# First norm by ScalarE and GpSimd, gates as rounded products, earlier bank choices and a last batch by row tiles in a decoder block with gated cross-attention

## The reference, cut to what matters

```python
# x (16, 256, 256), ctx (16, 77, 256)
h = layernorm(x + multihead(x, x, x, ..., causal=True), ln1_g, ln1_b)          # 16 heads of 16
h = layernorm(h + multihead(h, ctx, ctx, ..., causal=False), ln2_g, ln2_b)
h = layernorm(h + relu(h @ w1.T + b1) @ w2.T + b2, ln3_g, ln3_b)               # 1024 hidden
qp = h @ Wq + bq; kp = ctx @ Wk + bk; vp = ctx @ Wv + bv                       # one head of 256
y = softmax(qp @ kp.T / 16) @ vp
gate = concat(qp, y) @ Wg + bg
out = h + y * mask * sigmoid(gate)
# layernorm(z) = g * (z - mean) / (std + 1e-6) + b, std over d - 1
```

## Time and profile before

| what | value |
|---|---|
| median of 3 runs | 816.09 us (814.78 to 816.56) |
| the profiled execution's own time | 814.99 us |
| its span, first to last instruction | 812.6 us |
| mean granted TensorE clock | 0.978 |
| PE / PEld / DVE / ACT / POOL busy | 94% / 77% / 68% / 64% / 57% |

### The profile page before, as it was taken

One profiled execution on the slowest core, in us unless ns is written; L12 is line 12 of the kernel. 1 busy time (PEld: TensorE's weight loads), 2 busy tenths in 40 slices (PEclk: granted clock), 3 DMA queues, 4 the chain that ended last, 5 costly groups with the idle time before them and its releaser, 6 DMA issues.

```text
span 812.6 us, 19616 instructions
## 1 busy us (share of the span) xinstructions
PE 762.6 (94%) x7072; PEld 624.1 (77%) x7072; DVE 550.9 (68%) x1221; ACT 517.4 (64%) x1224; POOL 460.0 (57%) x582
## 2 busy tenths in 40 slices
PE   6998999999999998889699999999999999999986
PEld 4786778888877776556467889888888888988864
DVE  4435777878788988866878666686668544663453
ACT  5432466656565556555777888888777887855542
POOL 2403477767767676563346566656565588556330
PEclk9999999999999999896979999999999999999998
DMA  9687677987577674344322222222220100011132
GB/s 286 173 262 183 148 135 126 157 138 133 106 132 132 103 110 99 83 115 99 72 58 56 57 57 57 57 53 57 55 46 7 46 2 6 27 56 50 50 96 79
DMA packets 105304, 76.49 MB, mean 94 GB/s; under 512 B 43261, under 2 KB 101967, under 8 KB 104947
## 3 DMA queue, kind: packets, MB, share of 16 engines
q1 hardware_dynamic: 101850, 72.36, 41.7%
q10 hardware_dynamic: 3360, 2.90, 1.2%
HBM read 25.49 MB, written 11.42 MB: 45 GB/s over the span
## 4 chain that ended last, share of the span: by engine, by line
PE 51%; issue 14%; DVE 11%; POOL 10%; ACT 5%; DMA 1%; ACTq 0%; POOLq 0%; DVEq 0%
PE a_misc L89 11%; PE a_s L1039 5%; PE a_pair L89 5%; POOL c_hidden L1979 4%; PE a_pair L827 4%; PE a_s L803 4%; PE a_pair L845 4%; PE a_s L801 3%; PE a_pair L1126 3%; PE a_pair L1138 3%; DVE a_nm L1480 2%; PE a_s L1097 2%; DVE c_z L1590 1%; PE a_pair L999 1%; PE a_pair L848 1%
## 5 line engine op out<-in xcount | busy, mean ns | idle before, releaser
L1205 ACT ACTIVATE a_pT<-a_pair 128x512 f32<-128x512 f32 x192 | 113.7, 597 | 79.8 <-PE a_pair L827 72.4
L1979 POOL TENSOR_TENSOR c_hidden<-c_hid,c_hidden 128x256 fp32r<-128x256 f32 x128 | 94.5, 738 | 120.6 <-ACT c_hidden L1369 120.5
L1480 DVE TENSOR_REDUCE a_nm<-a_s 128x2 f32<-128x512 f32 (+1 forms) x192 | 126.9, 677 | 44.8 <-PE a_s L803 44.2
L1039 PE MATMUL a_s<-c_w,c_hidden 128*128 128x256 f32 x768 | 118.4, 293 | 0.7 <-DVE res L1731 0.7
L1335 ACT ACTIVATE a_pT<-a_pair 77x512 f32<-77x512 f32 x128 | 75.2, 589 | 64.4 <-PE a_pair L984 63.7
L1886 POOL TENSOR_SCALAR_AFFINE_SELECT a_pT<-a_pT 128x256 f32<-128x256 f32 (+1 forms) x192 | 91.4, 495 | 21.8 <-ACT a_pT L1205 21.4
L89 PE MATMUL a_pair<-c_fxh,c_w 128*128 128x256 f32 x512 | 99.9, 288 | 1.0 <-ACT c_hid L1361 1.0
L1039 PEld LDWEIGHTS a_s<-c_w,c_hidden 128*128 128x128 f32 x768 | 99.0, 190 | 1.7 <-issue 1.4
L1655 DVE TENSOR_REDUCE a_nm<-a_s 128x5 f32<-128x385 f32 (+1 forms) x96 | 55.3, 577 | 50.6 <-PE a_s L961 50.4
L89 PEld LDWEIGHTS a_pair<-c_fxh,c_w 128*128 128x128 f32 x512 | 79.3, 191 | 1.2 <-ACT c_hid L1361 1.2
L827 PE MATMUL a_pair<-a_sq,a_sk 98*128 98x256 bf16 (+1 forms) x512 | 75.1, 250 | 4.4 <-ACT a_pT L1205 3.7
(11 more groups left out here) (259 smaller groups left out, 1984.1 us busy)
## 6 DMA issues: line engine op xcount, KB each, us to landing
a_sq<-a_parts SPq DMA_DIRECT2D x96, 128.0 KB, 4.3
a_sk<-a_parts SPq DMA_DIRECT2D x96, 128.0 KB, 4.3
a_sq<-c_parts SPq DMA_DIRECT2D x96, 128.0 KB
x<-in_xT SPq DMA_DIRECT2D x16, 256.0 KB, 5.0
res<-in_x SPq DMA_DIRECT2D x16, 256.0 KB, 5.2
out<-g_fin SPq DMA_DIRECT2D x16, 256.0 KB, 2.1
a_sk<-kc_parts SPq DMA_DIRECT2D x96, 38.5 KB
g_vv<-vv_rows SPq DMA_DIRECT2D x16, 154.0 KB
```

Source lines behind the costliest of these rows:

```text
L1039: last = mt(down[:, qt * D:(qt + 1) * D], (hh, hl)[x](m)[:, qt * P:(qt + 1) * P], w2(y, m), start=m == 0 and qt == 0 and i == 0, stop=m == ...
L1205: nc.scalar.activation(pT[g % NPT][:], stps[g % 2][:], ACT.Exp).then_inc(s_exp, 1)
L1480: nc.vector.tensor_reduce(nm[c % 2][:, QT * heads[0] + qt:QT * heads[-1] + qt + 1:QT], sps[g % 2][:].rearrange("p (h k) -> p h k", h=len(h ...
L1979: nc.gpsimd.tensor_tensor(hl(m), hid[n % NHID][:], f32(hh(m)), ALU.subtract).then_inc(c_hl, 1)
```

## The change

The first norm becomes: DVE forms nmr1 = -mean/std for whole groups of batches at once, ACT does (res/std + nmr1) in one instruction per row tile, POOL multiplies by ln1_g, POOL adds ln1_b. The eight `weight_low` move from DVE to POOL. The gates are formed by `mm3` from a high and a low part of `gx` and of `wqg`. ACT and DVE make the parts of `gx`; the scores still use F32 `gx`. The stored gate weights double in size. `cross_values` alternates banks for its first seven groups. `LONE_H` and `LONE_XO` become 7 and 9. The last batch is mixed, gated, finished and stored by row tile.

```diff
@@ context_products
+            dve.wait_ge(s_wqgh, 1)
+            nc.vector.tensor_tensor(wqg[:, 1, :, :], two(fps[0]), f32(wqg[:, 0, :, :]), ALU.subtract).then_inc(s_wqgl, 1)
@@ banks
-    ND, GV, LONE_H, LONE_XO = 3, 4, 9, 11
+    ND, GV, LONE_H, LONE_XO = 3, 4, 7, 9
+    mixed_bank = lambda m: avps[m % 2] if m < SOLO_A else av_ps          # SOLO_A = 7
@@ PE cross_values
-                    atleast(pe, c_tr, rr // 2)
+                    atleast(pe, c_tr, m - 1 if m < SOLO_A else m)
@@ PE gates
+                pe.wait_ge(g_xl, c + 1)
                 for qt in range(QT):
-                    for kt in range(KT):
-                        last = mt(xo(c)[:, qt * 2 * D + D:(qt + 1) * 2 * D], gx[c % 3][:, kt, qt * P:(qt + 1) * P], wqg[:, kt, :],
-                                  start=kt == 0, stop=kt == KT - 1)
+                    last = mm3(nc.tensor, xo(c)[:, qt * 2 * D + D:(qt + 1) * 2 * D],
+                               lambda x, kt: (gxh, gxl)[x][c % 2][:, kt, qt * P:(qt + 1) * P], lambda y, kt: wqg[:, y, kt, :], range(KT))
@@ ACT
+            def first_normed(c):
+                act.wait_ge(c_nmr, 1 + (c >= B // 2) + (c >= B - 4))
+                atleast(act, c_h, c)
+                for qt in range(QT):
+                    n = QT * c + qt
+                    last = nc.scalar.activation(z1[:, qt, :], t.res[:, n, :], ACT.Identity, scale=t.rstd[:, n:n + 1], bias=nmr1[:, n:n + 1])
+                last.then_inc(c_zr, 1)
...
-                    centred_scale(n + 3, z1, c_zr, c_z, t.rstd)      # cross unit 1
+                if s == 6 and n > -4 or s == 7 and n == -4:
+                    first_normed(n + 4)
...
+                nc.scalar.activation(gxh[c % 2][:], gx[c % 3][:], ACT.Copy).then_inc(g_xh, 1)     # gated unit 3
@@ DVE
-                if s == 3:
-                    centred(n + 4)
-                if n in (-1, 0, 2, 3) and s in (3, 7):
-                    weight_low((-1, 0, 2, 3).index(n) * 2 + s // 7)
+                nc.vector.tensor_tensor(gxl[c % 2][:], gx[c % 3][:], f32(gxh[c % 2][:]), ALU.subtract).then_inc(g_xl, 1)   # gated unit 0, batch e - 1
@@ POOL
+                nc.gpsimd.tensor_tensor(z1[:], z1[:], ln1[0].unsqueeze(1).broadcast_to([P, QT, D]), ALU.mult).then_inc(c_weighted, 1)
...
                 if s == 0:
                     cross_o_low(n - 3)
+                    if n == -3:
+                        weighted_rows(0)
+                    shifted_rows(n + 3)
-                if s == 2:
-                    shifted_rows(n + 3)
...
+                if s == 7 and n > -4:
+                    weighted_rows(n + 4)
+                if n in (-1, 0, 2, 3) and s in (6, 7):
+                    weight_low((-1, 0, 2, 3).index(n) * 2 + s - 6)
@@ the last batch
+            def last_rows(qt):                                             # DVE, per row tile: gate, then finish
+                dve.wait_ge(g_fact, B + qt)
...
+            for qt in range(QT):
+                sp.wait_ge(g_fin, B + qt)
+                sp.dma_start(out[B - 1][:, qt, :], fin[(B - 1) % 2][:, qt, :]).then_inc(stored[(B - 1) % 2], 16)
```

More of the change, by code:

```diff
@@ L134, in context_products @@
     wkq = [sb(f"wkq{i}", [P, KT, D], F32R) for i in range(2)]
-    wqg = sb("wqg", [P, KT, D], F32)
+    wqg = sb("wqg", [P, 2, KT, D], F32R)
     parts = nc.alloc_sbuf_tensor_at("x_parts", [P, 3, B, KT, SC], BF16, offset=t.place["a_sq1"])
@@ L387, in _ @@
             act.wait_ge(s_wqg, 1)
-            nc.scalar.activation(wqg[:], two(fps[0]), ACT.Copy).then_inc(s_wqgc, 1)
+            nc.scalar.activation(wqg[:, 0, :, :], two(fps[0]), ACT.Copy).then_inc(s_wqgh, 1)
             for i in range(NTOK):
@@ L541, in causal_cross_feed_gated @@
     rootc = sb("rootc", [P, 3], F32)
-    rstd2 = sb("rstd2", [P, NT], F32)
+    rstd2, nmr1 = sb("rstd2", [P, NT], F32), sb("nmr1", [P, NT], F32)
     sps = [ps(f"s{i}", 512) for i in range(2)]
@@ L583, in causal_cross_feed_gated @@
     gvv = [gat(f"vv{i}", [SCE, 2 * D], F32, *p) for i, p in enumerate((("a_sq0", 0), ("a_sq0", half), ("a_sq1", 0)))]
-    wqg = gat("wqg", [P, KT, D], F32, "a_sq1", half)
-    gx = [gat(f"x{i}", [P, KT, S], F32, *p) for i, p in enumerate((("a_sq2", 0), ("a_sq2", 2 * quarter), ("a_sq3", 0)))]
+    wqg = gat("wqg", [P, 2, KT, D], F32R, "a_sq1", half)
+    gx = [gat(f"x{i}", [P, KT, S], F32, "a_sq2", i * quarter) for i in range(3)]
+    gxh, gxl = ([gat(f"{n}{i}", [P, KT, S], F32R, *p[i]) for i in range(2)]
+                for n, p in (("xh", (("a_sq2", 3 * quarter), ("a_sq3", 0))), ("xl", (("a_sq3", quarter), ("a_sq1", quarter)))))
     gate = [gat(f"gate{i}", [P, QT, D], F32, "a_sq3", (2 + i) * quarter) for i in range(2)]
@@ L778, in _ @@
                 sp.dma_start(gvv[c][SC:SCE], d.row).then_inc(g_row, 16)
-            sp.dma_start(wqg[:].rearrange("p k c -> p (k c)"), d.wqg).then_inc(g_wqg, 16)
-            for c in range(B):
+            sp.dma_start(f32(wqg[:].rearrange("p x k c -> p (x k c)")), d.wqg).then_inc(g_wqg, 16)
+            for c in range(B - 1):
                 if c + ND < B:
@@ L1446, in gate_tanh, with gate_tanh_last @@
                 nc.scalar.activation(gate[c % 2][:], xo(c)[:].rearrange("p (q c) -> p q c", q=QT)[:, :, D:2 * D], ACT.Tanh, scale=0.5).then_inc(g_fact, 1)
+            def gate_tanh_last(qt):
+                act.wait_ge(g_xo, B + qt)
+                atleast(act, g_gated, B - 2)
+                nc.scalar.activation(gate[(B - 1) % 2][:, qt, :], xo(B - 1)[:, qt * 2 * D + D:(qt + 1) * 2 * D], ACT.Tanh,
+                                     scale=0.5).then_inc(g_fact, 1)
             def gated_slot(e, k):
@@ L1451, in gated_slot @@
                         gated_one()
-                    gate_tanh(e - 2)
+                    if e - 2 < B - 1:
+                        gate_tanh(e - 2)
+                    if e - 2 == B - 1:
+                        for qt in range(QT):
+                            gate_tanh_last(qt)
                     p_copy(e - 1)
@@ L1580, in causal_slot @@
                     residual(n - 3)
-            def centred(c):
-                if not real(c):
-                    return
-                if c == 0:
-                    dve.wait_ge(s_xl, B - 1)
-                atleast(dve, c_h, c)
-                for qt in range(QT):
-                    n = QT * c + qt
-                    nc.vector.scalar_tensor_tensor(z1[:, qt, :], t.res[:, n, :], t.mv[:, n, 0:1], ln1[0], ALU.subtract,
-                                                   ALU.mult).then_inc(c_z, 1)
             def centred2(c):
@@ L1693, in cross_turn_av @@
                 atleast(dve, c_on, n)
-                nc.vector.transpose(tr[0][:], av_ps[:]).then_inc(c_tr, 1)
+                nc.vector.transpose(tr[0][:], mixed_bank(n)[:]).then_inc(c_tr, 1)
                 dve.wait_ge(c_tr, n + 1)
@@ L1798, in shares, with gated_x_low @@
                                         ALU.mult).then_inc(g_p, 1)
+            def gated_x_low(c):
+                if not real(c):
+                    return
+                if c == 0:
+                    stacks_dead(dve, 3)
+                dve.wait_ge(g_xh, c + 1)
+                atleast(dve, g_gates, c - 1)
+                nc.vector.tensor_tensor(gxl[c % 2][:], gx[c % 3][:], f32(gxh[c % 2][:]), ALU.subtract).then_inc(g_xl, 1)
             def gate_x(c):
@@ L1839, in gated_slot @@
                         gated_constants()
-                    finish(e - 3, 0)
+                    if e - 3 < B - 1:
+                        finish(e - 3, 0)
+                    if e - 3 == B - 2:
+                        finish(e - 3, 1)
                 if k == 1:
-                    gate_x(e - 2)
+                    if e - 2 < B - 1:
+                        gate_x(e - 2)
+                    if e - 2 == B - 1:
+                        for qt in range(QT):
+                            last_rows(qt)
                     gated_maxes(e)
-                if k == 2:
+                if k == 2 and e - 3 < B - 2:
                     finish(e - 3, 1)
@@ L1847, in gated_slot @@
                     shares(e)
+                if k == 0:
+                    gated_x_low(e - 1)
             for stage, n, s in order:
```

100 lines of the change are left out of this document (69 added, 31 removed).

## The result

The changed kernel takes 809.61 us, the median of five executions (804.25 to 810.47), beside 816.09 before: a ratio of 0.9908, with a 95% interval from 0.988 to 0.9935. Over all of them the mean is 808.4 (11 executions), against 817.3 for the kernel before (76): 9.0 us faster, where 20 had been forecast. Beside the kernel before in the same comparison the means differ by 7.6 in the first and by 9.7 in the second.

What follows compares the result with a forecast made beforehand. PE bounds the kernel, except where causal and cross slots interleave (261 to 450 us), where PE waits mostly for DVE. Stretch -15.0 (-11.0 - 2.0 - 8.0 + 6.0), gates -3.5, end -1.5: -20.0, so 796 us; range 784 to 812, own range 787 to 804.

Steps and rivals of the forecast that it cites:

- rival A: Interleaved stretch: DVE not the bound, freed time becomes waits for scores and exponentials; banks give 4; 810 us; chance 0.18.
- The DVE work that goes: Interleaved causal and cross slots (261 to 450 us): removed DVE instructions end 11.0 of PE's 16.5 us waits; bounds 4, 16.5.
- ACT: Same interleaved stretch: a third of the 6.1 us that PE waits for ACT's exponentials goes, 2.0; bounds 0 and 4.
- The clock: Same stretch: lost clock falls like PE's idle time, 55% of 15.1 us, so 8.0 come back; bounds none and 12.
- The POOL work: Same stretch: POOL's new multiplies and low parts (24.4 us of work) cost 6.0 us; bounds 1 and 14.
- The two joints I named: Cross slots -1 and 0, units 6 and 7: POOL's queued work makes PE wait 2 us at each.
- The cross slots after it: Cross slots without causal ones, after the interleaved stretch: PE full, still 21.0 us each, no change forecast.
- caught chains: Interleaved stretch: new POOL instructions slow some of DVE's short chains, 2.0 us, part of the 6.0 for POOL.
- The gates: Gate products: 0.29 us less per batch, none at batch 10; 3.5 us taken in all; bounds 1 and 4.6.
- The wait for `g_xl` at batch 10: Batch 10's gates: wait for the new low part replaces the wait for g_gated, so that batch gains nothing.
- The end: From the last mix to the end: half-size finishes save 1.1 us, smaller last store 0.4; sum -1.5, bounds 0.6 and 2.2.
- Context part, XO and H banks: Context part's extra subtract and DRAM traffic: nothing, 1 us if uncovered; the bank changes LONE_XO and LONE_H: no gain.

Runs made afterwards that it cites:

- e13: Kernel before with only the first norm changed and POOL's multiply by its weight left out: 805.56 us, ratio 0.986.
- e15: Changed kernel without POOL's multiply by the first norm's weight and with the weight low parts back on DVE: 805.77 us, ratio 0.9851.
- e9: Changed kernel with POOL's multiply by the first norm's weight left out: 806.29 us, ratio 0.9862.
- e3: Kernel before with only the two alternating banks for the first seven products with the values: 815.62 us, ratio 0.9977.
- e12: Changed kernel with the first norm back on DVE and ACT as before: 812.61 us, ratio 0.9948.
- e6: Changed kernel with POOL's weight multiply at cross unit 0 of its own slot and the bias at unit 2: 805.25 us, ratio 0.9846.
- e4: Kernel before with only the gates changed: three rounded products, their high and low parts, LONE_H 7 and LONE_XO 9: 814.61 us, ratio 0.9972.
- e10: Changed kernel with the weight multiply at unit 0, the last deviation chain behind the shares, batch 13's second row tile finished earlier: 801.38 us, ratio 0.9813.
- e1: Kernel before with only the first norm changed, POOL's weight multiply included: 812.35 us, ratio 0.9935.
- e2: Kernel before with only the eight weight low parts moved from DVE to POOL: 814.40 us, ratio 0.9964.

## Why the prediction was wrong

The direction held, and so did the places; the size was more than twice what came. The measured 809.61 lies within 784 to 812 only because that range was drawn out to take in rival A's 810; it is outside the forecast's own 787 to 804. By its steps:

- **The DVE work that goes: the failed step.** "I take two thirds of 16.5, 11.0." With nothing new on GpSimd DVE's waits fell by 4.6 and 5.2 (e13, e15, with L1590 gone) and PE's idle time by 5.9 and 5.6; by 6.5 with the low parts gone too (e9). The bound of a quarter (4) was nearer than the value taken. The nine waits on the maxima are queues on DVE, as I read them, but six of them stand behind other work: over all of DVE's 16.5, the trace of before has a removed instruction in front of 7.1. Of what went, 2.2 (e15) came back at the next instruction that PE needs from DVE. The 4.0 at the banks was inside the relief as I had it: in e13, with one bank, it fell to 1.0. The new banks alone (e3) end it too, but there the turn of the cross maxima waits instead.
- **ACT: about right.** 2.0 were forecast; its waits fell by 1.5 (e13) and 2.4 (e15).
- **The clock: right for the relief, wrong for the whole.** 8.0 were forecast, and 8.0 came back in both runs without GpSimd's new work. In the whole 5.4 came back in the mean of three profiles, 7.9, 2.3 and 6.1 one by one; that the new waits let it fall again is likely, but the same kernel scatters by more than the difference. The step that tied it to idle time in proportion (55% less idle, 55% less clock loss) fails in form: idle fell by a quarter and the clock's loss by half. In e3 the idle time rose by 2.3 and the loss fell by 5.7. What the dips hang on instead is not shown.
- **The POOL work: right in size as far as one profile tells,** 6.0 forecast, 5.1 measured (2.6 of them through the clock), net of what DVE gained by the low parts' leaving. The two joints I named were not the ones: the worst is cross slot 3, units 6 and 7, where I had the products "two units or more ahead of their users". They are, but DVE is not. POOL and DVE in the first profile:

```profile
386.52 1.27 POOL L2045 TENSOR_TENSOR c_w<-c_raw,c_w 128x512 fp32r<-128x512 f32 x1
387.75 1.26 POOL L1984 TENSOR_TENSOR c_z<-c_z,ln_g 128x512 f32<-128x512 f32 x1
388.97 1.27 POOL L2045 TENSOR_TENSOR c_w<-c_raw,c_w 128x512 fp32r<-128x512 f32 x1
```

```profile
386.71 1.10 DVE L1649 TENSOR_SCALAR a_var<-mv 128x2 f32<-128x2 f32 x1
387.85 1.19 DVE L1651 TENSOR_SCALAR a_root<-a_var 128x2 int32<-128x2 int32 x1
388.95 0.43 DVE L1734 STREAM_TRANSPOSE a_o<-a_on 128x256 f32<-128x256 f32 x1
389.41 0.28 DVE L1712 TENSOR_TENSOR a_mT<-a_misc,a_mT 32x128 bf16<-32x128 f32 x1
```

  Each of the two tiny instructions ends with POOL's (0.15 and 0.17 at 525, where POOL is idle), and L1712, for which PE waits 2.4, is two places behind. The same wait of 2.4 stands in e9 and e12, which have the low parts on POOL and no multiply.
- **The cross slots after it: 1.3 more, forecast at nothing.** "Cross slots still 21.0" held for all but the one from 10 to 11, where the multiply meets the deviation chain (e6). The forecast's 2.0 for caught chains was for the stretch alone.
- **The gates: right where they were costed, absent elsewhere.** 0.29 for each of nine batches (e4). The six at the end gave nothing, where I had taken 0.9 off for all together; so 2.5 in the tail, not 3.5. The wait for `g_xl` at batch 10 came as written, at 2.4. That the clock may fall behind it was not in the sum; it is 0.7 to 1.0 us from batch 9's gates to batch 15's, and most of why gates and end together gave 2.5 in the whole and not 3.5.
- **The end: -1.0 for -1.5.** From the last mix to the end 8.3 became 7.3. The missing 0.5 is a wait of 0.63 of batch 15's first `fin` for the store of batch 13, whose second row tile is finished only behind `gate_x` of batch 14; with that moved up it is 6.7 (e10), 1.6 less, as forecast.
- **Context part, XO and H banks:** nothing, as forecast; between the first landmark and that of causal batch 11 the changed kernel is 0.3 shorter.

In sum: forecast -15.0, 0, -3.5 and -1.5; measured -8.4, +1.3, -2.5 for gates and end, and -0.3 ahead of it all, -9.9 from single profiles where the means differ by 9.0. Of the rivals A came nearest in its number (810), but not in its mechanism: the banks gave 1.4 rather than 4, and DVE's relief was real. (That DVE itself waits for L803 and L961, which A has from the earlier trace rows, does not stand in those rows; the view of DVE's waits has it, 6.0 and 15.2 from 261 to 450.)

The rule of the Trainium skill cited in the prediction ("GPSIMD Engine Reference") names as victims VectorE instructions with two SBUF inputs or in a 2-port performance mode. The 0.95 above is of the first kind; the 1.10 and 1.19 have one input, and whether they ran in such a mode no row shows. By that rule alone the move would have been a loss; the runs make the new norm a gain of 4 to 5 us (e12, e1), its price on GpSimd included.

Left open: why e2's time fell by 2 to 3 us where its profile shows 1.2; the share of the low parts in the 5.1; and what decides how far the clock falls, since the same kernel's stretch scatters by 5.6 us through it.

## What to carry to other kernels

A wait that an engine ends is not relief just because that engine gets less to do: look in the timeline at what the engine did before the instruction that ends the wait, count only waits with the work that goes in front of them, and expect a part of them to come back at the next instruction that is needed. When elementwise work moves to GpSimd, look at which tiny VectorE instructions stand in a chain beside its new place, since each may grow from 0.16 to 1.2 us; another unit of the same slot was worth 2.9 us here (e6). On TensorE the same wait of 2.4 to 2.6 us was followed by no fall of the clock in one profile and by 13 us at its lower level in another, so take several executions, and cut the span at fixed pieces of work, before a difference of a few us is put down to a change.

## What the runs showed of the hardware

A 128x2 VectorE instruction that runs 0.15 to 0.17 us alone took 1.10 and 1.19 beside two-input GpSimd instructions of 1.27, and ended when these did, although these two (`TENSOR_SCALAR`) have one input. In the kernel before, 40 VectorE instructions of 128x2 or 128x8 (reductions and aggregates left out) took over 0.6 us, and in the changed kernel 44; each of them ends within 0.04 us of a GpSimd instruction's end.

After the same wait of 2.4 to 2.6 us before batch 10's gates TensorE's granted clock stayed at 2.4 GHz, fell to 1.2 for 3 us, or for 13, in kernels whose program is the same there (e4; the changed kernel; e15). The Trainium skill ("TensorE: Matmul & The Clock Gate", Part 1: The HAM clock gate) says of a kernel's first matmuls that the gate's timing runs free of the program and so varies between runs of one kernel; these profiles fit that, in the middle of a kernel. From batch 9's gates to batch 15's the price was 0.7 us (3 us at the lower level) and 5.4 (13 us).
